# Keys and values of three pairs projected in three rounded passes, keys loaded in larger pieces, every order rewritten

## The reference

```python
def attn(query, ctx):                       # 32 query heads, 8 key/value heads, 16 wide
    Q = query @ Wq + bq; K = ctx @ Wk + bk; V = ctx @ Wv + bv
    w = softmax(einsum("bhgqd,bhkd->bhgqk", Q, K) / 4)
    return einsum("bhgqk,bhkd->bhgqd", w, V) @ Wo + bo
def ffn(x):                                 # 512 -> 1792 -> 512, scales per 128x128 block
    return (silu(x @ w1.T) * (x @ w3.T)) @ w2.T
x = x + tanh(g_xattn) * attn(layernorm(x), ctx)
x = x + tanh(g_ffn) * ffn(layernorm(x))
```

## Time and profile before

| | |
|---|---|
| median of 3 runs | 387.36 us (384.52 to 388.12) |
| the profiled execution | 385.39 us, of which span 383.7 us |
| mean granted TensorE clock | 0.996 of full speed |
| PE busy | 367.8 us, 96% |
| DVE / ACT / POOL busy | 258.4 / 184.8 / 153.9 us |
| attention with the first feed-forward pieces | 0 to about 168 us |
| feed-forward alone | about 168 to 383.7 us |
| moved by DMA | 34.96 MB, queue of SP 29.3% of 16 engines' time |

### The profile page before, as it was taken

How to read it: one execution, slowest core, us unless ns; L and a number is a source line. 1 busy time by engine, 2 the same in 40 slices (tenths; PEclk the granted TensorE clock), 3 DMA queues, 4 the chain that set the end, 5 groups by cost and what they waited for, 6 DMA issues and landing times.

```text
span 383.7 us, 6007 instructions
## 1 busy us (share of the span) xinstructions
PE 367.8 (96%) x2212; PEld 299.2 (78%) x2212; DVE 258.4 (67%) x418; ACT 184.8 (48%) x319; POOL 153.9 (40%) x130
## 2 busy tenths in 40 slices
PE   8997989999999999989999999999999999999996
PEld 6776967887777778668888888888888888888885
DVE  2856879999899777897777777453844445454434
ACT  2671679879999774442243223232423323322320
POOL 8701689999999985443344333000000000000000
PEclk9998999999999999999999999999999999999999
DMA  7999698757431500790000000000300000000002
GB/s 260 354 268 242 163 231 263 179 119 207 116 85 15 179 1 2 302 422 17 0 0 0 0 0 0 0 0 0 111 0 0 0 0 0 0 0 0 1 0 109
DMA packets 15604, 34.96 MB, mean 91 GB/s; under 512 B 2176, under 2 KB 7296, under 8 KB 14784
## 3 DMA queue, kind: packets, MB, share of 16 engines
q1 hardware_dynamic: 15296, 34.18, 29.3%
q10 hardware_dynamic: 288, 0.52, 0.4%
HBM read 26.04 MB, written 7.34 MB: 87 GB/s over the span
## 4 chain that ended last, share of the span: by engine, by line
PE 55%; DVE 1%; issue 0%
PE ps L1835 19%; PE ps L1837 18%; PE ps L1836 18%; DVE X L1270 1%; DVE w13L L1264 0%
## 5 line engine op out<-in xcount | busy, mean ns | idle before, releaser
L1835 PE MATMUL ps<-x2HL,w13H 128*128 128x512 f32 x224 | 89.2, 398 | 0.0
L1837 PE MATMUL ps<-x2HL,w13L 128*128 128x512 f32 x224 | 88.5, 395 | 0.0
L1836 PE MATMUL ps<-x2HL,w13H 128*128 128x512 f32 x224 | 88.4, 395 | 0.0
L479 POOL TENSOR_TENSOR PL<-E,PH 128x512 f16<-128x512 f32 x64 | 75.0, 1192 | 6.7 <-ACT E L756 3.3
L490 POOL TENSOR_TENSOR wres<-wres,gsc 128x1536 f32<-128x1536 f32 x14 | 42.1, 3004 | 45.9 <-DVE hf L1283 45.9
L778 ACT ACTIVATE T<-ps 128x512 f32<-128x512 f32 x28 | 16.7, 597 | 78.3 <-PE ps L1837 78.3
L786 ACT ACTIVATE hH<-hf 128x512 fp32r<-128x512 f32 x28 | 17.7, 632 | 68.0 <-DVE hf L1283 68.0
L1837 PEld LDWEIGHTS ps<-x2HL,w13L 128*128 128x128 f32 x224 | 42.0, 187 | 10.4
L1836 PEld LDWEIGHTS ps<-x2HL,w13H 128*128 128x128 f32 x224 | 42.0, 188 | 9.7
L1835 PEld LDWEIGHTS ps<-x2HL,w13H 128*128 128x128 f32 x224 | 42.0, 188 | 9.6
L1276 DVE SCALAR_TENSOR_TENSOR A<-T,ps 128x512 f32<-128x512 f32 x28 | 19.2, 685 | 43.7 <-ACT T L778 43.7
(11 more groups left out here) (100 smaller groups left out, 629.7 us busy)
## 6 DMA issues: line engine op xcount, KB each, us to landing
wres<-in_wff SPq DMA_DIRECT2D x14, 768.0 KB, 7.8
Qst<-qscr SPq DMA_DIRECT2D x21, 256.0 KB, 4.4
ct<-in_ctxt SPq DMA_DIRECT2D x8, 256.0 KB, 4.2
X<-in_x SPq DMA_DIRECT2D x8, 256.0 KB, 4.9
x2HL<-kscr SPq DMA_DIRECT2D x24, 64.0 KB, 3.6
qscr<-QTH SPq DMA_DIRECT2D x3, 512.0 KB, 2.8
qscr<-QTL SPq DMA_DIRECT2D x3, 512.0 KB, 4.0
out<-X SPq DMA_DIRECT2D x6, 256.0 KB, 2.5
```

What stands on the lines that cost most here:

```text
L479: pool.tensor_tensor(PL[:, g % NL, :], E[:, g % NE, :], PH[:, g, :], ALU.subtract).then_inc(pL_ok, 1)
L1835: pe.matmul(out_ap, aH, bH, start=start, stop=False)
L1836: pe.matmul(out_ap, aH, bL, start=False, stop=False)
L1837: return pe.matmul(out_ap, aL, bH, start=False, stop=stop)
```

## The change

- The keys and values of pairs 1, 2 and 3 are projected by a new `project_kv`, three fp32r matmuls on split weights and split context. Pair 0 keeps `project_kv32`. The split context of a pair stands in the part of `x2HL` whose tokens come later (`ctx_pair`). `context_high` (ScalarE, tiles 2 to 7) and `context_low` (VectorE tile 2, GpSimd tiles 3 to 7) are new, as are the splits of the key weights (VectorE) and of the value weights (ScalarE, GpSimd).
- Keys go out in three parts (the high part twice, as part 0 and part 2) and come in by one transfer for each parity of the heads in place of six: 12 stores and 8 loads in place of 8 and 24. A third semaphore `kg_out` is awaited by `k_high`.
- A row of the query scratch is padded by 32 elements (`PITCH`), so that a full `queries_in` reads elements of 2 KB in place of 8 KB. The output bias comes as an array of 128 rows (`biaso`) in place of one row sent to all partitions.
- All lists are new. ScalarE takes all key and query high parts; VectorE takes three `v_bias`, all four `v_first`, `clear_keys(0)`, three `x2_high` and two `add_out_bias` (0 and 1). GpSimd takes seven `shift` and five `shift2`; its `add_out_bias` 2, 3 and 4 stand ahead of the first `weight_low`, number 5 in batch 5, number 6 in batch 7; `scale(0)` stands in batch 2, `scale(1)` in batch 3 and `scale(2)` behind the last `weight_low`, and their loads stand later in SP's list. In TensorE's list the keys of pair 3 come behind the queries of pair 1.
- At the end `x2` of batches 5, 6 and 7 is rounded on VectorE, and the low half of w2 stands ahead of that of h.

```diff
 NCT, NKST, NQ = 4, 4, 3
+PITCH = GJ * P + 32
 NWARM = 12
-GATE, SC = DM, DM + 2
+GATE, SC = 0, 2
...
+        def ctx_pair(n, low):
+            s = TWO * (n // 2 % 2)
+            return x2HL[:, low, :, s:s + TWO]
+
+        def ctx_of(n, low):
+            return ctx_pair(n, low)[:, :, n % 2 * P:(n % 2 + 1) * P]
 
...
-        def keys_out(eng, p, low):
-            eng.dma_start(kscr[p, low], r32((KTL if low else KTH)[:])).then_inc((kh_out, kl_out)[low], 16)
-
-        def keys_in(eng, p, t, gg):
+        def keys_out(eng, p, t):
+            eng.dma_start(kscr[p, t], r32((KTL if t == 1 else KTH)[:])).then_inc((kh_out, kl_out, kg_out)[t], 16)
+
+        def keys_in(eng, p, gg):
             s = (NBATCH - NKST + 2 * p % NKST) * P
-            r = 32 * t + DH * gg
-            eng.dma_start(r32(kall(r, r + DH)[:, gg:KVH:2, s:s + TWO]),
-                         kscr[p, t % 2, 64 * gg:64 * gg + 64].rearrange("(r h) n -> r h n", h=PAIRS)).then_inc((k_in0, k_in1)[p % 2], 16)
+            eng.dma_start(r32(x2HL[gg:ROWS:2].rearrange("p a k n -> p (a k) n")[:, gg:KVH:2, s:s + TWO]),
+                         kscr[p].rearrange("t (d g h) n -> g (t d) h n", g=2, h=PAIRS)[gg]).then_inc((k_in0, k_in1)[p % 2], 16)
 
         def queries_out(eng, p, low, j0, j1, done):
             eng.dma_start(qscr[p, low, :, :, j0 * P:j1 * P].rearrange("b r n -> r b n"),
                          r32((QTL if low else QTH)[:, :, j0:j1, :]).rearrange("r b j q -> r b (j q)")).then_inc(done, 16)
 
         def queries_in(eng, n, t, done):
-            eng.dma_start(r32(Qst[32 * t:32 * t + 32, slot(n), :, :]).rearrange("r h n -> r (h n)"),
-                         qscr[n // 2, t // 2, n % 2].rearrange("(r h) n -> r (h n)", h=PAIRS)).then_inc(done, 16)
+            eng.dma_start(r32(Qst[32 * t:32 * t + 32, slot(n), :, :]),
+                         qscr[n // 2, t // 2, n % 2, :, 0:GJ * P].rearrange("(r h) n -> r h n", h=PAIRS)).then_inc(done, 16)
 
         def queries_part(eng, n, t, j0, j1, done):
             eng.dma_start(r32(Qst[32 * t:32 * t + 32, slot(n), :, j0 * P:j1 * P]),
@@ -263,160 +272,149 @@
 
         @block.sync
         def _(sp):
-            sp.dma_start(raw[:, V0:Q0], wproj[:, V0:Q0]).then_inc(wv_in, 16)
+            sp.dma_start(raw[:, K0:V0], wproj[:, K0:V0]).then_inc(wk_in, 16)
             context_in(sp, 0)
             context_in(sp, 1)
+            sp.dma_start(raw[:, V0:Q0], wproj[:, V0:Q0]).then_inc(wv_in, 16)
...
+            tokens_in(sp, 3)
+            context_in(sp, 5)
             sp.wait_ge(kT_H, 1)
+            keys_out(sp, 0, 2)
             keys_out(sp, 0, 0)
-            tokens_in(sp, 3)
             sp.wait_ge(kT_L, 1)
             keys_out(sp, 0, 1)
+            tokens_in(sp, 6)
+            tokens_in(sp, 5)
+            tokens_in(sp, 4)
+            context_in(sp, 6)
             out_weights_in(sp)
+            sp.wait_ge(kg_out, 16)
+            sp.wait_ge(kh_out, 16)
             sp.wait_ge(kl_out, 16)
-            keys_in(sp, 0, 1, 1)
-            context_in(sp, 5)
-            sp.wait_ge(kh_out, 16)
-            keys_in(sp, 0, 0, 1)
-            keys_in(sp, 0, 0, 0)
-            tokens_in(sp, 6)
-            keys_in(sp, 0, 2, 1)
-            tokens_in(sp, 5)
-            sp.wait_ge(qT_H_dve, 1)
-            sp.wait_ge(qT_H, 1)
+            keys_in(sp, 0, 1)
+            sp.wait_ge(kT_L, 2)
+            keys_out(sp, 1, 1)
+            sp.wait_ge(qT_H, 2)
             queries_out(sp, 0, 0, 0, 2, qh_outa)
+            keys_in(sp, 0, 0)
+            keys_out(sp, 1, 0)
+            keys_out(sp, 1, 2)
             sp.wait_ge(qT_L, 2)
             queries_out(sp, 0, 1, 0, 2, ql_outa)
...
+            def context_low(n):
+                pool.tensor_tensor(ctx_of(n, 1), tokens(n), r32(ctx_of(n, 0)), ALU.subtract).then_inc(ctL_ok, 1)
...
-            clear_keys(0)
-            clear_keys(1)
+            pool.wait_ge(wvH_ok, 1)
+            weights_low(V0, Q0, wvL_ok_pool)
             pool.wait_ge(ve1_ok, 1)
             root(0)
+            pool.wait_ge(ctH_ok_act, 2)
+            context_low(3)
             pool.wait_ge(ve1_ok, 2)
             root(1)
-            pool.wait_ge(wqH_ok_dve, 1)
+            pool.wait_ge(rs1_ok, 2)
+            shift(1)
+            pool.wait_ge(wqH_ok, 1)
             weights_low(Q0, QH, wqL_ok_pool)
...
+            context_low(6)
+            pool.wait_ge(rs1_ok, 6)
+            shift(5)
+            pool.wait_ge(woH_ok, 1)
+            weights_low(O0, PW, woL_ok)
+            pool.wait_ge(mH_ok, 1)
+            max_low(0, 2)
+            pool.wait_ge(ctH_ok_act, 6)
+            context_low(7)
             pool.wait_ge(mH_ok, 2)
             max_low(2, 4)
-            max_low(0, 2)
-            weights_low(O0, PW, woL_ok)
+            pool.wait_ge(ve1_ok, 7)
+            root(6)
+            pool.wait_ge(bo_ok, 1)
+            add_out_bias(2)
+            add_out_bias(3)
+            pool.wait_ge(rs1_ok, 7)
+            shift(6)
+            add_out_bias(4)
             pool.wait_ge(PH_ok, 1)
             weight_low(0)
...
+            pool.wait_ge(ve1_ok_pool, 1)
+            root(7)
+            pool.wait_ge(E_ok, 9)
             weight_low(0)
-            scale(0)
...
-            pool.wait_ge(bo_ok, 1)
-            add_out_bias(0)
             pool.wait_ge(PH_ok, 16)
             weight_low(7)
...
+            pool.wait_ge(E_ok, 21)
+            pool.wait_ge(pv_ps, 17)
             weight_low(4)
+            scale(0)
             pool.wait_ge(PH_ok, 22)
             weight_low(5)
-            pool.wait_ge(E_ok, 23)
...
+            scale(1)
             pool.wait_ge(E_ok, 29)
-            pool.wait_ge(pv_ps, 25)
             weight_low(4)
-            add_out_bias(4)
...
+            weight_low(1)
+            add_out_bias(5)
+            pool.wait_ge(E_ok, 43)
+            weight_low(2)
             pool.wait_ge(mH_ok, 8)
...
-            root2(4)
             pool.wait_ge(ve2_ok, 6)
             root2(5)
+            pool.wait_ge(rs2_ok, 6)
+            shift2(5)
+            scale(2)
             add_out_bias(7)
             pool.wait_ge(ve2_ok, 7)
             root2(6)
...
+            def context_high(n):
+                act.wait_ge(ct_in[n % NCT], 16 * (n // NCT + 1))
+                act.activation(ctx_of(n, 0), tokens(n), ACT.Copy).then_inc(ctH_ok_act, 1)
 
...
+            weights_high(wv_in, V0, Q0, wvH_ok)
+            context_high(2)
+            act.wait_ge(k_ps, 1)
+            k_high(W0)
+            context_high(3)
             act.wait_ge(v_ps, 1)
             v_bias(W2)
-            act.wait_ge(vt_ps, 1)
-            v_first(0, W2)
-            act.wait_ge(k_ps, 1)
-            k_high(W0)
             act.wait_ge(nb1_ok, 1)
             normalise(0)
...
+            def context_low(n):
+                dve.tensor_tensor(ctx_of(n, 1), tokens(n), r32(ctx_of(n, 0)), ALU.subtract).then_inc(ctL_ok_dve, 1)
+
+            def add_out_bias(n):
+                dve.tensor_tensor(X[:, n, :], X[:, n, :], boT[:], ALU.add).then_inc(xb_ok_dve, 1)
...
+            weights_high(wk_in, K0, V0, wkH_ok_dve)
+            clear_keys(0)
+            dve.wait_ge(wkH_ok_dve, 1)
+            weights_low(K0, V0, wkL_ok)
             statistics(0)
             dve.wait_ge(stats1, 1)
             mean(0)
-            statistics(1)
             dve.wait_ge(mean1, 1)
             epsilon(0)
+            dve.wait_ge(rs1_ok, 1)
+            shift(0)
+            dve.wait_ge(ctH_ok_act, 1)
+            context_low(2)
+            dve.wait_ge(kT_H, 1)
+            k_low(W0)
+            statistics(1)
             dve.wait_ge(stats1, 2)
             mean(1)
-            dve.wait_ge(v1_ok_act, 1)
-            v_residue(0, W2)
-            dve.wait_ge(rs1_ok, 1)
-            shift(0)
+            dve.wait_ge(vt_ps, 1)
+            v_first(0, W1)
             dve.wait_ge(mean1, 2)
             epsilon(1)
-            dve.wait_ge(kT_H, 1)
-            k_low(W0)
-            dve.wait_ge(rs1_ok, 2)
...
+            def project_kv(bank, n, w0, k0, k1):
+                for k in range(k0, k1):
+                    w = slice(w0 + k * KVD, w0 + (k + 1) * KVD)
+                    m = three(bank[:, 0:TWO], WpH[:, w], WpL[:, w], ctx_pair(n, 0)[:, k, :], ctx_pair(n, 1)[:, k, :], k == 0, k == KB - 1)
+                return m
...
+            project_kv32(W0, 0, K0, 0, 2)
             project_kv32(W2, 0, V0, 0, 2)
+            project_kv32(W0, 0, K0, 2, 4).then_inc(k_ps, 1)
             project_kv32(W2, 0, V0, 2, 4).then_inc(v_ps, 1)
-            project_kv32(W0, 0, K0, 0, 2)
             pe.wait_ge(vT_ok, 1)
-            turn_v(W2).then_inc(vt_ps, 1)
-            project_kv32(W0, 0, K0, 2, 4).then_inc(k_ps, 1)
-            project_kv32(W1, 2, V0, 0, 2)
-            project_kv32(W1, 2, V0, 2, 4).then_inc(v_ps, 1)
+            turn_v(W1).then_inc(vt_ps, 1)
             pe.wait_ge(kT_L, 1)
             pe.wait_ge(xn_ok, 1)
             turn4(W0, xn).then_inc(xT_ps, 1)
-            pe.wait_ge(vT_ok, 2)
```

(14 more changed lines are left out.)

1692 lines of the change are left out of this document (839 added, 853 removed).

## The result

| kernel | median us | the kernel before beside it | ratio, 95% interval |
|---|---|---|---|
| changed kernel | 387.96 (385.43 to 391.98, 20 runs) | 385.92 (384.02 to 388.12, 20 runs) | 1.0047 [1.0027, 1.0067] |

The change makes the kernel about 0.5% slower: within 1% of the kernel before, 4.8 us above the forecast of 383.2 and just outside its range. (Medians are over all runs; the ratio leaves disturbed ones out, so the two can differ by a few tenths of a per cent.) More runs also put the kernel before at 385.92, not at the 387.36 that the forecast was laid on; on that scale the forecast was 381.7. The profiled execution of the changed kernel took 387.66 us with a span of 385.9; before it was 385.39 and 383.7, so the two traces show the difference, 2.2 us.

A forecast was written before the change was run, and what follows sets the result against it. TensorE was taken as the bound, busy 367.8 of 383.7 us, with attention paced by GpSimd as much. Terms -2.0 - 1.6 - 0.6 = -4.2 us took 387.36 to 383.2 us, range 378.5 to 387.6.

The forecast's parts named there:

- Part 1: Key and value projections: three fp32r passes instead of fp32 save 1.9 us of TensorE, counted inside the -2.0 us at scores(2,0).
- Part 2: Start: the first query projection waits for pair 1's split context and starts at 16.4 us, 0.8 us later.
- Part 3: First query waits: scores(0,0) stays at 31.2 us, batch 2's queries return earlier, scores(2,0) starts 2.2 us earlier; net -2.0 us.
- Part 4: GpSimd's list in its never-idle stretch, 60 to 125 us: net 7.0 us less work, taken as worth -1.6 us.
- (b): Rival: GpSimd's relief is lost as scaling 0 waits for late weights; 385.4 us, chance 0.28.
- (d): Rival: bias additions ahead of GpSimd's first low half end late and delay all 64; slower, 391.5 us at 55 us; chance 0.08.
- Part 5: Key loads merged per parity and 2 KB elements: SP gains 7 us but isn't late; transfer size effects counted as nothing.
- Part 6: End, before the first two down projections: gaps shrink from 0.56 to 0.4 and 1.64 to 1.2 us; -0.6 us.
- (e): Rival: a later start passes through both query trips and the change gives nothing; 387.4 us, chance 0.04.

The follow-up runs named there:

- e9: Changed kernel with both query orders repaired and 8 KB query reads, but keys and values of pairs 2 and 3 projected in fp32 again: 384.74 us, ratio 0.9971.
- e4: Changed kernel with SP's queue reordered at 30 us: one batch 1 query read before the last context block, output bias behind all three: 385.60 us, ratio 0.9969.
- e8: e4 with six spare 128x512 subtractions (about 7.1 us) added to GpSimd's list between 60 and 105 us: 388.99 us, ratio 1.0059.
- e12: Changed kernel with both query orders repaired, 8 KB query reads, and GpSimd's scale(3) waiting for the last low half of x2: 382.52 us, ratio 0.9867.
- e7: e4 with the query rows read in 8 KB pieces instead of 2 KB: 386.25 us, ratio 1.0024.

## Why the prediction was wrong, step by step

**Part 1** (-1.9 us of TensorE) was right in kind, a little too large: a half group fell from 0.86 us to between 0.70 and 0.80, some 1.3 us for twelve. As the text said, it counts only through the next wait; e9 shows that wait swallowing it.

**Part 2**: the first query projection started at 16.67 us, forecast 16.4, before 15.61. Right.

**Part 3** (-2.0) failed, and its failing step is one that isn't in it: scores(1,0). scores(0,0) came at 31.19 as forecast, and the queries of pair 1 were projected even sooner than at 38.9. But I followed only the queries of batch 2. Those of batch 1 were issued from 31.31 us on, no sooner than before (31.27), behind the last context block and the output bias, which is 256 KB in place of a broadcast row and stood far later in the old list; they took 5.3, 5.7 and 7.4 us to land. TensorE was ready for scores(1,0) at 37.4 us in place of 41.1 and waited 2.67 us there, with the lower clock behind it. scores(2,0) gained 0.6 us instead of 2.2. e4 moves the bias load and puts one query read ahead of the context block, and has 2.4 us back.

**Part 4** (-1.6) was right about GpSimd and wrong in taking the relief for time. Between scores(2,0) and scores(5,3) the kernel before took 44.27 us and the changed one 42.48, 1.8 us less. That looks like a hit and isn't one: 1.6 us of it is work that the new list has outside this stretch. TensorE's small waits for other engines in this stretch did fall, from 1.27 to 0.12 us. In their place stand waits for queries at scores(3,0), (4,0) and (5,0), 1.33 us together, where the kernel before had none:

```profile
63.88 0.71 PE L1942 MATMUL ps<-x2HL,Qst 96*128 96x256 f32 x4 [0.32 <-DMA Qst<-qscr]
...
75.72 0.72 PE L1942 MATMUL ps<-x2HL,Qst 96*128 96x256 f32 x4 [0.47 <-DMA Qst<-qscr]
...
87.39 0.72 PE L1942 MATMUL ps<-x2HL,Qst 96*128 96x256 f32 x4 [0.54 <-DMA Qst<-qscr]
```

The relief passed to the next limit, the transfers. What it is worth where they don't hold TensorE no run shows; e8 prices the load put back, 2.8 us for 7.1. Rivals (b) and (d) are out: scaling 0 started at 78.22 without a wait for weights, and the three bias additions ended before the first low half, which came at 47.84, 1.2 us later than before.

**Part 5** was counted as nothing, and for the size of the pieces no run could show more. But its heading covered the trips of all queries, and there the sum has its hole: no part followed the queries of batch 6. The diff moves `project_q(W1, 3, ...)` from before scores(5,0) to behind the turned maxima, 2.7 us later, and 13 us on that is a wait of 2.65 us and 1.3 us of lower clock. From scores(5,3) to scores(7,0) the traces differ by 6.1 us: 3.1 us are work that stood elsewhere in the old list, 2.1 us the longer wait, 1.3 us the clock, which comes out within 0.4 us. Before, TensorE had waited at this place too, though for keys and shortly:

```profile
102.84 0.74 PE L1881 MATMUL ps<-x2HL,Qst 96*128 96x256 f32 x4 [0.54 <-DMA x2HL<-kscr]
```

This row says that scores(6,0) had no slack for anything later. It was in the trace before the forecast and I didn't weigh it.

**Part 6** (-0.6) failed in its first term. I expected a wait of 0.4 us, it was 1.52; the second was 1.01 (forecast 1.2). Together they grew by 0.3 us in place of falling by 0.6. The place at which VectorE subtracts w2's low part moved under GpSimd's scaling 3, and became 2.91 us long. I had cited that very effect, with its row, for the bias additions, and not applied it to the end; e12 shows it.

**The sum.** The forecast had -2.0, -1.6 and -0.6. By the same marks the traces have -0.6 up to scores(2,0), -1.8 to scores(5,3), +6.1 to scores(7,0) and -1.5 to the second down projection: +2.2. The first down projection, expected near 157 us, came at 163.83. Two trips of queries not followed and one blocked subtraction outweigh what parts 1 and 4 gave. None of the rivals describes this. The nearest is (e), for its time alone. The method's fault was to cost the parts that the change speaks of, and not to list every transfer whose producer moved.

**Open.** Whether 2 KB or 8 KB pieces are better; what the larger key reads do to the landing of the queries beside them; how much the three passes and GpSimd's relief bring once no wait for queries hides them; and why e7 isn't faster than e4.

## What to carry to other kernels

When an order is made anew, list for each transfer when its data are produced, what stands ahead of it in its queue and when it is wanted, in both lists: a projection 2.7 us later can cost nothing for 10 us and then 4 us at once. Before two traces are compared between two marks, count the work that each list has between them. A store moved earlier brings nothing while it is queued behind a load that waits for a free slot. And before a VectorE operation with two inputs in SBUF is placed on the path, look at which long GpSimd operation runs beside it.
